# The attention pass's weighted one-hots, written in two bytes with the weight in three parts

## The reference, cut to what matters

```python
h = x @ W
alpha = leaky_relu(a_s[src] + a_d[dst] + a_e, 0.2)
m = segment_max(alpha, dst, num_segments=n)
ex = exp(alpha - m[dst])
w = ex / segment_sum(ex, dst, num_segments=n)[dst]
out = segment_sum(w[:, None] * h[src], dst, num_segments=n) + b
```

## Time and profile before

| | |
|---|---|
| median of 3 runs | 2506.21 us (2505.8 to 2514.34) |
| the profiled execution | 2507.93 us, its span 2506.1 us |
| PE busy | 1840.6 us, 73% |
| DVE busy | 1400.4 us, 56% |
| ACT busy | 1022.3 us, 41% |
| POOL busy | 976.7 us, 39% |
| first attention pass, about | 1308 to 1645 us |
| second attention pass, about | 1802 to 2138 us |

### The profile page before, as it was taken

One profiled execution on the slowest core, in us unless ns is written; L12 is line 12 of the kernel. 1 busy time (PEld: TensorE's weight loads), 2 busy tenths in 40 slices (PEclk: granted clock), 3 DMA queues, 4 the chain that ended last, 5 costly groups with the idle time before them and its releaser, 6 DMA issues. The chain is left out here.

```text
span 2506.1 us, 43046 instructions
## 1 busy us (share of the span) xinstructions
PE 1840.6 (73%) x13196; PEld 1444.0 (58%) x13196; DVE 1400.4 (56%) x4673; ACT 1022.3 (41%) x2637; POOL 976.7 (39%) x995
## 2 busy tenths in 40 slices
PE   4788787777875389996168888952688889397792
PEld 4677676666765367665155666742556667265462
DVE  5567666666665799994075444541754445502306
ACT  2444444444442556663006554620155556300202
POOL 1666666656553200001606666235166662200000
PEclk8899988899887699997559888975699999699896
DMA  6655555555550235543232111023211110344340
GB/s 194 173 168 176 163 172 169 165 160 180 158 164 25 81 129 198 189 180 112 50 97 58 37 38 36 22 74 77 72 56 37 38 38 16 119 176 178 118 176 28
DMA packets 154957, 281.76 MB, mean 112 GB/s; under 512 B 28583, under 2 KB 98221, under 8 KB 151444
## 3 DMA queue, kind: packets, MB, share of 16 engines
q1 hardware_dynamic: 114990, 196.63, 23.5%
q0 software_dynamic: 35456, 79.88, 11.6%
q10 hardware_dynamic: 4278, 2.42, 0.4%
HBM read 228.82 MB, written 50.00 MB: 111 GB/s over the span
## 5 line engine op out<-in xcount | busy, mean ns | idle before, releaser
L1007 POOL DMA_INDIRECT gated_rows<-p_tab,src_idx x416 | 429.5, 1032 | 325.3 <-DVE gated_pre L1177 180.9
L1369 POOL DMA_INDIRECT ring<-table,src_idx x384 | 373.8, 973 | 323.0 <-POOLq L2276 130.6
L2086 PE MATMUL bank<-counts,mean_xs 128*128 128x416 bf16 (+2 forms) x1350 | 222.8, 325 | 64.7 <-DVE mean_xs L1694 64.7
L1177 DVE TENSOR_TENSOR gated_pre<-bank,gated_rows 128x512 f32<-128x512 f32 x208 | 142.2, 684 | 188.4 <-remote 111.6
L1036 PE MATMUL bank<-gated_wide_q,gated_comb 128*128 128x256 f32 x832 | 237.6, 412 | 3.2 <-issue 3.1
L1544 PE MATMUL bank<-attention_counts,h_sb 128*128 128x232 f32 (+1 forms) x900 | 205.1, 357 | 26.1 <-ACT attention_counts L1509 15.2
L1544 PEld LDWEIGHTS bank<-attention_counts,h_sb 128*128 128x128 f32 x900 | 165.8, 200 | 94.9 <-ACT attention_counts L1509 30.0
L1105 ACT ACTIVATE gated_sig<-gated_pre 128x512 f32<-128x512 f32 x208 | 131.1, 630 | 215.8 <-DVE gated_pre L1177 183.6
L2086 PEld LDWEIGHTS bank<-counts,mean_xs 128*128 128x128 bf16 x1350 | 127.1, 98 | 151.4 <-issue 71.0
L1532 PE MATMUL bank<-attention_wide_a,scratch 128*128 128x300 f32 x448 | 171.8, 468 | 47.2 <-issue 28.5
L1533 PE MATMUL bank<-attention_wide_b,scratch 128*128 128x400 f32 x448 | 202.0, 534 | 0.0
(11 more groups left out here) (403 smaller groups left out, 4080.8 us busy)
## 6 DMA issues: line engine op xcount, KB each, us to landing
counts<-count_tabs SPq DMA_DIRECT2D x16, 2675.0 KB, 9.3
scratch<-in_edge_attr_dram SPq DMA_DIRECT2D x51, 512.0 KB, 3.9
count_tabs<-mean_counts SPq DMA_DIRECT2D x8, 2675.0 KB, 10.9
gated_relr<-rel_rows SPq DMA_DIRECT2D x104, 128.0 KB
gated_ids<-id_rows SPq DMA_DIRECT2D x26, 512.0 KB
gated_wide_q<-q_tab SPq DMA_DIRECT2D x208, 64.0 KB
attend_hot_lo<-low_hots SPq DMA_DIRECT2D x52, 256.0 KB, 3.0
gated_ea<-in_edge_attr_dram SPq DMA_DIRECT2D x51, 256.0 KB
```

Source lines behind the costliest of these rows:

```text
L1007: pool.indirect_dma_start(out=rows[:, q % TICKS, c, :], out_offset=None, in_=p_tab, in_offset=bass.IndirectOffsetOnAxis(ap=src_idx[:, b, j ...
L1177: dve.tensor_tensor(flat(pre[:, q % 2, :, :]), PRE[q % 2][:, :], flat(rows[:, q % TICKS, :, :]), ALU.add).then_inc(pre_ready, 1)
L1369: pool.indirect_dma_start(out=rows[:, n % RING, j, :], out_offset=None, in_=table, in_offset=bass.IndirectOffsetOnAxis(ap=src_idx[:, gathe ...
L2086: mm = pe.matmul(BANKS_D[k % ND][:, 0:width], xs[:, m // 3, m % 3, :], counts[:, s % 2, m // 3, at:at + width], start=(m == 0), stop=(m == ...
```

## The change

`lo` becomes three 2-byte tables per chunk instead of one of four bytes. Each holds the one-hot times one of three 2-byte parts of the weight; the three parts add up to the weight. `wide_a` and `wide_b` are written in two bytes. PE multiplies each of the three with the same wide operand and sums in PSUM. At the start of each pass DVE cuts the weights (128 x 416) in parts with five instructions. DVE makes the first part's table itself, in one instruction per chunk with two operands per partition (the low bits and the weight's part); ACT makes the second and third from `plain`. For the gathered batches nothing changes in type, but every other batch's `hot` is now made wholly by DVE (four instructions instead of one), and ACT has no part in it.

```diff
-            plain = sb("plain", [P, LR, 2, P], BF16)
-            wide_a, wide_b = sb("wide_a", [P, WR, NT * WA]), sb("wide_b", [P, WR, NT * WB])
+            lo = scratch[:, row_at + 3 * P:row_at + 3 * P + LR * 3 * P].bitcast(BF16).rearrange("p (r c i n) -> p r c i n", r=LR, c=2, i=3)
+            parts, part_b = sb("parts", [P, 2, NB, J]), sb("part_b", [P, NB, J], BF16)
+            plain = plain_all[:, :].rearrange("p (r c n) -> p r c n", r=LR, c=2)
+            wide_a, wide_b = sb("wide_a", [P, WR, NT * WA], BF16), sb("wide_b", [P, WR, NT * WB], BF16)
@@ ScalarE, weigh_lo(n)
-                            ins = act.activation(lo[:, n % LR, c, :], plain[:, n % LR, c, :], ACT.Copy, scale=w_c[:, b, 2 * k + c:2 * k + c + 1])
+                            for i in range(2):
+                                ins = act.activation(lo[:, n % LR, c, 1 + i, :], plain[:, n % LR, c, :], ACT.Copy, scale=parts[:, i, b, 2 * k + c:2 * k + c + 1])
@@ ScalarE, around the steps
+                    act.wait_ge(cut_in_parts, 5)
-                    weigh_hot(0)
-                            if n in G_AT and G_AT[n] + 1 < NGB:
+                            if n in G_AT and G_AT[n] + 1 < NGB and by_act(G_AT[n] + 1):
                                 weigh_hot(G_AT[n] + 1)
@@ TensorE, count(n)
+                        pe.wait_ge(first_ready, n + 1)
-                        pe.matmul(to[:, :, 0:WA], lo[:, n % LR, 0, :], wide_a[:, n % WR, :], start=True, stop=False, skip_group_check=True)
-                        pe.matmul(to[:, :, OFF:WP], lo[:, n % LR, 1, :], wide_b[:, n % WR, :], start=False, stop=True,
-                                  skip_group_check=True).then_inc(counted, 1)
+                        for i in range(3):
+                            pe.matmul(to[:, :, 0:WA], lo[:, n % LR, 0, i, :], wide_a[:, n % WR, :], start=(i == 0), stop=False, skip_group_check=True)
+                        for i in range(3):
+                            mm = pe.matmul(to[:, :, OFF:WP], lo[:, n % LR, 1, i, :], wide_b[:, n % WR, :], start=False, stop=(i == 2), skip_group_check=True)
+                        mm.then_inc(counted, 1)
@@ VectorE, make_hot(n); by_act(n) is n % 2 == 1
+                        if not by_act(n):
+                            for j in range(J):
+                                ins = dve.tensor_scalar(hot[:, n % HB, j, :], iota[:, :], rel[:, b, j:j + 1], w_tab[:, b, j:j + 1], ALU.is_equal, ALU.mult)
+                            ins.then_inc(hot_whole, 1)
+                            return
@@ VectorE, make_lo(n), behind the instruction that writes plain
+                        reach(dve, counted, n - LR + 1)
+                        for c in range(2):
+                            ins = dve.tensor_scalar(lo[:, n % LR, c, 0, :], lo_iota[:, :], src_lo[:, b, 2 * k + c:2 * k + c + 1],
+                                                    part_b[:, b, 2 * k + c:2 * k + c + 1], ALU.is_equal, ALU.mult)
+                        ins.then_inc(first_ready, 1)
@@ VectorE, at the start of the pass
+                    halves = flat(w_c[:, :, :]).bitcast(BF16)[:, 0:NB * J]
+                    cuts(dve.tensor_copy(part_b[:, :, :], w_c[:, :, :]))
+                    cuts(dve.tensor_tensor(rest, flat(w_c[:, :, :]), part_b[:, :, :].rearrange("p b j -> p (b j)"), ALU.subtract))
+                    cuts(dve.tensor_copy(halves, rest))
+                    cuts(dve.tensor_copy(part[0], halves))
+                    cuts(dve.tensor_tensor(part[1], rest, part[0], ALU.subtract))
```

More of the change, by code:

```diff
@@ L1378, in attention_pass @@
             lo_at = HB * J * W
-            row_at = lo_at + LR * 2 * P
-            lo = scratch[:, lo_at:row_at].rearrange("p (r c n) -> p r c n", r=LR, c=2)
+            plain_all = sb("plain", [P, LR * 2 * P], BF16)
+            row_at = lo_at
+            lo = scratch[:, row_at + 3 * P:row_at + 3 * P + LR * 3 * P].bitcast(BF16).rearrange("p (r c i n) -> p r c i n", r=LR, c=2, i=3)
+            parts, part_b = sb("parts", [P, 2, NB, J]), sb("part_b", [P, NB, J], BF16)
+            rest = plain_all[:, :].bitcast(F32)[:, 0:NB * J]
+            plain = plain_all[:, :].rearrange("p (r c n) -> p r c n", r=LR, c=2)
             pass_row, end_row, carry_row = [scratch[0:1, row_at + k * P:row_at + k * P + n] for k, n in enumerate((NB, NB, NB + 1))]
-            plain = sb("plain", [P, LR, 2, P], BF16)
-            wide_a, wide_b = sb("wide_a", [P, WR, NT * WA]), sb("wide_b", [P, WR, NT * WB])
+            wide_a, wide_b = sb("wide_a", [P, WR, NT * WA], BF16), sb("wide_b", [P, WR, NT * WB], BF16)
             counts = sb("counts", [P, TB, NT, A_COLS])
@@ L1392, in attention_pass @@
             lo_ready, wide_ready, counted, copied, joined = sem("lo_ready"), sem("wide_ready"), sem("counted"), sem("copied"), sem("joined")
-            cleared, plain_ready = sem("cleared"), sem("plain_ready")
+            hot_whole = sem("hot_whole")
+            cleared, plain_ready, first_ready, cut_in_parts = sem("cleared"), sem("plain_ready"), sem("first_ready"), sem("cut_in_parts")
             scanned, carried, aux_ready, aux_stored = sem("scanned"), sem("carried"), sem("aux_ready"), sem("aux_stored")
@@ L1432, in attention_pass, with by_act @@
             assert len(added_at) == ALL
+            def by_act(n):
+                return n % 2 == 1
             def finished(engine):
@@ L1478, in weigh_lo @@
                         for c in range(2):
-                            ins = act.activation(lo[:, n % LR, c, :], plain[:, n % LR, c, :], ACT.Copy, scale=w_c[:, b, 2 * k + c:2 * k + c + 1])
+                            for i in range(2):
+                                ins = act.activation(lo[:, n % LR, c, 1 + i, :], plain[:, n % LR, c, :], ACT.Copy, scale=parts[:, i, b, 2 * k + c:2 * k + c + 1])
                         ins.then_inc(lo_ready, 1)
                     def weigh_hot(n):
-                        act.wait_ge(hot_made, n + 1)
+                        act.wait_ge(hot_made, n // 2 + 1)
                         b = gathered_batch(n)
@@ L1550, in sum_gathered @@
                         pe.wait_ge(rows_in[n % RING], 64 * (n // RING + 1))
-                        pe.wait_ge(hot_ready, n + 1)
+                        if by_act(n):
+                            pe.wait_ge(hot_ready, n // 2 + 1)
+                        else:
+                            pe.wait_ge(hot_whole, n // 2 + 1)
                         if n > 1:
@@ L1617, in _ @@
                     link = chain(dve, v)
+                    cuts = chain(dve, cut_in_parts)
+                    part = [parts[:, i, :, :].rearrange("p b j -> p (b j)") for i in range(2)]
+                    halves = flat(w_c[:, :, :]).bitcast(BF16)[:, 0:NB * J]
[4 more added lines that the diff above has]
+                    cuts(dve.tensor_tensor(part[1], rest, part[0], ALU.subtract))
                     for n in range(AHEAD):
```

## The result

The changed kernel took 2515.8 us, the kernel before beside it 2506.2 us (medians of 20 runs each). The ratio is 1.0046, with an interval of 1.0031 to 1.0062: slower by 10 us by the medians and 12 by the ratio, inside the 0.5% that I had called no change. The forecast was 2464 us, with a range that ended at 2502. It was wrong.

A forecast was written before the change was run, and what follows sets the result against it. PE was taken to set the pace of both attention passes, beside 53 us of waits per pass. Per pass -40 (counts) + 3 (cut) + 15 (fuller engines) = -22 us, twice -44: 2507.93 to 2464 us, range 2415 to 2502.

The forecast's parts named there:

- PE's counts: PE's products per window: six two-byte instructions at 0.90 us replace four at 1.23, saving about 40 us per pass.
- Cut of the weights: Five uncovered chained instructions at the start of each pass, before everything else: 3 us more per pass.
- ACT and DVE: Busy times of both engines in a pass: ACT from 184 to 235 us, DVE from 162 to 238.
- What the fuller engines give back: Ring of PE, ACT and DVE in a pass: less slack, charged 15 us per pass, ends 0 and 40.
- a pass near 336 us with ACT hardly idle: One of the signs in the attention passes that would show the forecast to be wrong.
- Late signals: Waits in each pass where PE's signal comes late: 53 us per pass, expected to stay, nothing charged.
- The sum: Terms of both attention passes: -40 + 3 + 15 = -22 us per pass, -44 in all, giving 2464 us.
- The gain is lost in the ring: Rival: ACT or DVE sets the passes' pace, charge 30 us instead of 15, 2494 us; chance 0.15.
- The late signals go too: Rival: half of the passes' late-signal waits vanish with the four-byte counts, 2411 us; chance 0.14.
- POOL's gathers are held up: Rival: each POOL instruction in a pass waits for a whole DVE instruction, 2476 us; chance 0.04.
- DVE becomes the bound: Rival: DVE's two-operand instructions cost far over 0.342 us, a pass takes some 345 us, 2526 us total; chance 0.09.

The follow-up runs named there:

- b_same: The kernel before, unchanged, run again for its trace at the lower level: 2120.4 us, ratio 1.0007.
- a_act2_nog: The changed kernel without ScalarE's weighings of the third part and without row gathers after the eighth batch: 2081.9 us, ratio 0.9824 to the kernel before.
- a_best3: The changed kernel with VectorE making all one-hots whole, the cut in two steps and auxiliary gathers last, third run, lower level: 2106.2 us, ratio 0.9940.
- a_act2: The changed kernel without ScalarE's weighings of the third part; TensorE reads the second part twice: 2109.0 us, ratio 0.9952 to the kernel before.
- a_pe1: The changed kernel without TensorE's products of the second and third part: 2129.1 us, ratio 1.0058 to the kernel before.
- a_hotdve: The changed kernel with VectorE making every gathered batch's one-hots whole: 2114.3 us, ratio 0.9978 to the kernel before.
- a_best2: The changed kernel with VectorE making all one-hots whole, the cut in two steps and auxiliary gathers last, second run, upper level: 2513.5 us, ratio 1.0014.
- a_nog2: The changed kernel without row gathers after the eighth batch, second run, at the upper level: 2429.7 us, ratio 0.9679 to the kernel before.
- b_nog2: The kernel before without row gathers after the eighth batch, second run, at the upper level: 2418.2 us, ratio 0.9641 to it unchanged.
- a_hotcut: The changed kernel with VectorE making all one-hots whole and the cut in two steps, lower level: 2110.5 us, ratio 0.9963 to the kernel before.
- b_aux: The kernel before with the auxiliary gathers moved behind the last batch of rows, upper level: 2523.9 us, ratio 0.9960 to it unchanged.
- b_nog: The kernel before without row gathers after the eighth batch, at the lower level: 2117.7 us, ratio 0.9994 to it unchanged.

## Why the prediction was wrong, by its own steps

**PE's counts**: right in kind, a little too large. A count takes 0.89 us against my 0.90, but the one that it replaces was 1.18 us and not the 1.23 of a single place in the earlier trace rows. PE's timeline in b_same, where nothing comes between:
```profile
1604.87 0.67 PE L1532 MATMUL bank<-attention_wide_a,scratch 128*128 128x300 f32 x2
1605.37 0.83 PE L1533 MATMUL bank<-attention_wide_b,scratch 128*128 128x400 f32 x2
1606.05 0.95 PE L1544 MATMUL bank<-attention_counts,h_sb 128*128 128x232 f32 x4
```
So 0.29 x 112 = 32 us a pass could be had, not 37, and not the 40 that the sum took by scaling it to the mean clock. From first to last copy a_act2_nog got 21 of them (236.6 us against 257.9) and a_best3 24 (233.7): they are real once the others are relieved.

**Cut of the weights**: right, 3.16 us a pass against 3; shown by the starts in the table.

**ACT and DVE**: the prices were good, or too high. ACT was busy for 223 us against 235 (448 weighings for 142.4 us), DVE for 204 against 238: a two-operand instruction is 0.321 us long, and the next can start after 0.22. ACT got nothing back for the two-byte output: a weighing took 391 ns with four bytes and with two. The Trainium skill (ScalarE: Activation LUTs, "What ACT_TABLE_LOAD costs") has one rate for both types, and the trace agrees.

**What the fuller engines give back**: this is the step that failed. I charged 15 us a pass for the tighter ring and had 40 as the end (nothing of PE's gain is kept). At the lower level, where nothing else disturbs, the measured charge is the end itself: from first to last copy 259.1 and 260.5 us against 257.3 and 257.9, so PE's 32 us went in whole, and 2 us more: 34 where I had 15. The reason is not the slack that I worked out for single steps. I had the numbers: ACT "tied up" for 255 us a pass, PE with 219 us of work and some of it at the lower clock. I set ACT's 255 against a pass of 314 us, of which 53 were waits that I didn't understand, and called the difference room. Against PE's own work there was none. Experiments a_act2, a_pe1 and a_hotdve show it from three sides. The sign that I had written for it, a pass near 336 us with ACT hardly idle, would have missed it at the upper level: ACT is idle there for 119 of 342 us, much of it in wait for late signals.

**Late signals**: half right. I left them as they were, and their sum nearly stayed: blocks 0 to 6 of the second pass took 64.7 us more at the upper level than at the lower in the kernel before (289.2 against 224.5) and 66.5 in the changed one (297.2 against 230.8), where I had 53. But I took them for a term that stands beside PE's work, as if what PE saves came off the pass all the same. At the upper level blocks 0 to 6 go at the pace in which TensorE's signals get through while GpSimd gathers; 45 us a pass of the kernel before go with the gathers (334.2 to 289.7), and even with ScalarE relieved nothing of the saving came through (a_best2). The gain was hidden twice. a_nog2 against b_nog2 shows that ScalarE's ring is enough to hide it. That the late signals are enough as well rests on a_best2 alone, which also has the auxiliary gathers moved.

**The sum** by what was measured, for the lower level: 2 x 3.16 us of start, 1.8 + 2.6 us between first and last copy, together 10.7 us; the medians differ by 2127.0 - 2118.4 = 8.6, the ratio gives 10.8. At the upper level the cut is 6.3 of the 12 us; I can't divide the rest between ring and signals.

**The rivals.** "The gain is lost in the ring" was the nearest in mechanism, with ACT as the engine, but priced at half the loss. "The late signals go too" did not happen: they stayed with the counts in two bytes. "POOL's gathers are held up" was wrong as put: a gather took 986 ns against 977 while DVE's busy share rose from 48% to 60%. Whatever the rule of the shared ports in the Trainium skill (SBUF — State Buffer, "SBUF: two separate sides") does here, it is no more than these 9 ns a gather. That a pass can't be shorter than GpSimd's chain of gathers, 193 x 1.28 = 247 us by my own numbers, I had not used as a floor for the gain. "DVE becomes the bound" did not happen: its two-operand instruction took 0.321 us, and a_hotdve, which gives DVE more work still, was faster.

What stays open: why one kernel has two levels (the record numbers the chip of each set, and number 1 stands beside sets at either level, so the number alone does not decide it), by what way GpSimd's gathers hold TensorE's signals and instructions at the upper one, and whether a_hotcut, without the moved gathers, gains there too.

## What to carry to other kernels

Before an engine is spared, write down the work and the handovers of every other engine in the same loop, and compare them with the spared engine's own work, not with the length of the loop: waits that you can't explain are no reserve. Then ask for the next floor as well, here GpSimd's chain of gathers with its drain, which even the best version ran into. And where one engine's signal comes later than its record says, first look at what else runs at that moment.

## What the runs showed of the hardware

The kernel before takes 2118 us or 2506 to 2532 us, with the same instructions. The 18% are not in the prices of the instructions. DVE's group of L1177 in the stage with the other gathers, from the page of the kernel before and from that of b_same:
```profile
L1177 DVE TENSOR_TENSOR gated_pre<-bank,gated_rows 128x512 f32<-128x512 f32 x208 | 142.2, 684 | 188.4 <-remote 111.6
```
```profile
L1177 DVE TENSOR_TENSOR gated_pre<-bank,gated_rows 128x512 f32<-128x512 f32 x208 | 142.8, 686 | 75.8 <-PE bank L1036 45.8
```
684 and 686 ns are one price; the idle time ahead of it is 188.4 and 75.8 us. At the upper level a run of 25 back-to-back gathers, 31 us, held TensorE's signal of a count for 27 us (b_aux). At the lower level a run of 25 left ACT its 15 copies in 34 us (b_nog), and in the second pass of b_same all 193 gathers follow each other without a pause (0.31 us at most from the end of one to the next), and TensorE is busy for 194.84 of 195 us beside them. I had not expected that gathers touch a chain in which they have no part.
